# Attention probabilities split into halves in SBUF and transposed by DMA, in a cross-attention and two-expert network kernel

## The reference

```python
x = x + _L0_xattn_ref(_layernorm(x, axis=-1), ctx_1024, mask_Bx1xSxS2_ik0, mask_Bx1xS2_bk0, Wq, Wk, Wv, Wo, bo)
x = x + _L0_ffn_ref(_layernorm(x, axis=-1), gate_w, w1, b1, w2, b2, sw1, sb1, sw2, sb2)
# attention: sim = q k^T * SCALE, masked; attn = softmax(sim); out = attn v; out Wo^T + bo
# network: routing_output (relu network of the row's top-1 expert, plus the idle expert's bias path)
#          + shared (relu(xf @ sw1 + sb1) @ sw2 + sb2)
```

## Time and profile before

| | |
|---|---|
| median of 3 runs | 1881.85 us (1881.73 to 1882.95) |
| the profiled execution | 1883.23 us |
| its span | 1881.4 us |
| TensorE busy in the span | 1823.4 us, 97% |
| VectorE, ScalarE, GpSimd busy | 794.6, 821.2, 500.3 us |

### The profile page before, as it was taken

One profiled execution on the slowest core, in us unless ns is written; L12 is line 12 of the kernel. 1 busy time (PEld: TensorE's weight loads), 2 busy tenths in 40 slices (PEclk: granted clock), 3 DMA queues, 4 the chain that ended last, 5 costly groups with the idle time before them and its releaser, 6 DMA issues. The chain is left out here.

```text
span 1881.4 us, 33418 instructions
## 1 busy us (share of the span) xinstructions
PE 1823.4 (97%) x11516; PEld 1149.2 (61%) x11517; DVE 794.6 (42%) x1651; ACT 821.2 (44%) x1441; POOL 500.3 (27%) x475
## 2 busy tenths in 40 slices
PE   8989999999989999999999999999999999999997
PEld 6334444544656666666666666666666666666664
DVE  6977778777334343343433332222222222222222
ACT  3655555555333333335445544333333334333333
POOL 2047777776101111121100010222111121222111
PEclk9999999999989999999999999999999999999998
DMA  8235555555962333233345493812211112212100
GB/s 324 85 87 149 165 166 167 172 165 142 280 112 83 98 91 100 81 98 123 123 143 147 138 326 96 257 46 58 55 46 45 39 46 55 52 50 61 46 24 15
DMA packets 230151, 214.44 MB, mean 114 GB/s; under 512 B 130864, under 2 KB 172336, under 8 KB 229680
## 3 DMA queue, kind: packets, MB, share of 16 engines
q1 hardware_dynamic: 221120, 188.09, 34.9%
q0 software_dynamic: 8944, 25.19, 4.2%
HBM read 129.57 MB, written 59.02 MB: 100 GB/s over the span
## 5 line engine op out<-in xcount | busy, mean ns | idle before, releaser
L1058 PE MATMUL pS<-room_a,room_w 128*128 128x256 f16 (+1 forms) x6336 | 768.1, 272 | 8.4 <-issue 5.7
L1058 PEld LDWEIGHTS pS<-room_a,room_w 128*128 (+1 forms) x6336 | 612.9, 98 | 191.2 <-issue 18.0
L1089 DVE TENSOR_TENSOR room_a<-room_a 128x256 f16<-128x256 f32 (+1 forms) x528 | 235.2, 446 | 912.3 <-ACT room_a L1083 885.9
L1070 PE MATMUL pP<-room_w,room_a 128*128 (+1 forms) x1584 | 384.8, 380 | 9.2 <-DVE room_a L1089 9.2
L1081 ACT ACTIVATE room_a<-pS,room_b,sc 128x256 f32<-128x256 f32 (+1 forms) x272 | 151.7, 558 | 429.2 <-PE pS L1058 401.4
L1081 ACT ACTIVATE room_a<-pS,b1s,sc 128x256 f32<-128x256 f32 x256 | 144.2, 563 | 381.4 <-PE pS L1058 378.2
L1070 PEld LDWEIGHTS pP<-room_w,room_a 128*128 128x128 f16 x1584 | 155.0, 98 | 142.1 <-DVE room_a L1089 9.5
L1070 PE MATMUL pG<-room_w,room_a 128*128 128x512 f16 (+1 forms) x768 | 207.5, 379 | 0.4 <-DVE room_a L1089 0.4
L1070 PE MATMUL pO<-room_w,room_a 128*128 128x512 f16 (+1 forms) x768 | 207.6, 379 | 0.0
L1106 POOL TENSOR_TENSOR room_a<-room_a,room_b 128x512 f32<-128x512 f32 x32 | 42.7, 1354 | 535.8 <-DVE room_a L1097 535.8
L480 PE MATMUL pO<-room_w,room_b 128*128 (+1 forms) x768 | 172.7, 382 | 4.8 <-DVE room_b L692 4.7
(11 more groups left out here) (180 smaller groups left out, 1538.1 us busy)
## 6 DMA issues: line engine op xcount, KB each, us to landing
room_b<-in_w SPq DMA_DIRECT2D x64, 512.0 KB, 4.9
e_split<-room_b SPq DMA_DIRECT2D x64, 256.0 KB
room_w<-e_split SPq DMA_DIRECT2D x8, 2048.0 KB
rows_room<-in_x SPq DMA_DIRECT2D x32, 256.0 KB, 3.1
room_a<-in_sw SPq DMA_DIRECT2D x32, 256.0 KB, 4.3
room_b<-in_x SPq DMA_DIRECT2D x32, 256.0 KB, 4.1
s_split<-room_a SPq DMA_DIRECT2D x64, 128.0 KB, 3.8
x_scratch<-room_b SPq DMA_DIRECT2D x32, 256.0 KB, 4.2
```

The lines of the kernel that those rows point to most:

```text
L1058: mm = q.matmul(self.pH[j % 2][:, 0:rows], w[:, k, j * P:(j + 1) * P], zt[:, u, k, 0:rows], start=(n == 0), stop=(n == 3 * KC - 1))
L1070: mm = q.matmul(self.pY[u][r][:, :], h[:, j % self.HR, r * P:(r + 1) * P], w[:, j, :], start=(j == 0 and n == 0), stop=(j == HC - 1 and n ...
L1089: q.tensor_tensor(self.hl[:, j % self.HR, 0:rows], self.hf[:, j % self.HR, 0:rows], self.hh[:, j % self.HR, 0:rows], ALU.subtract).then_in ...
```

## The change

The transposes of the probabilities on TensorE and the identity go. `hi_p` and `lo_p` now read `s` in SBUF and write both halves side by side to `prs`; SyncE turns them with one DMA, `turn_p`, into `pT` (two buffers), and `attend` reads that. `hi_p` waits until the turn of the block before has been read out. On VectorE `lo_p` now stands ahead of `residual`; on SyncE `turn_p` stands first in a block's list, and `load_w1_w2(0)` moves behind the turn of the last block. For the first blocks, one `lo_x` and one `shifts` are placed earlier. The order list is blanked before the loop, from 33 rows of 128 zeros, and no longer from `inv`. Small buffers of the shared network change place, and VectorE waits for `lo_z` of block 30 (`z_done`) before it writes `rb1`.

```diff
+                prs = take([2, HEADS, KEYS], F16)
-                pTh = take([PAIRS, P], F16)
-                pTl = take([PAIRS, P], F16)
+                pT = take([2, 2 * PAIRS, P], F16)
...
+                    sp.wait_ge(S["zeros"], 1)
+                    sp.dma_start(order_d.rearrange("(s p) one -> s (p one)", p=P), zeros).then_inc(blank, 16)
...
+                    def turn_p(e, g, u):
+                        e.wait_ge(S["pl"], count(g, u))
+                        at_least(e, S["att"], count(g, u) - 2)
+                        e.dma_start(pT[:, u % 2, :, :], prs[:, :, :, :].rearrange("p l h k -> p (l h k)"), transpose=True).then_inc(S["pT_in", u % 2], 16)
...
                         for u in range(N):
+                            step(sp, g, u, 0, turn_p)
+                            if isinstance(g, int) and N * g + u == SUB - 1:
+                                sp.wait_ge(S["sim"], SUB)
+                                load_w1_w2(0)
                             step(sp, g, u, 3, turn_x)
...
                             snet.transpose(sp, t, z_d[t * TOK:(t + 1) * TOK, :])
-                        sp.wait_ge(S["sim"], SUB)
-                        load_w1_w2(0)
...
-                    def t_p(e, g, u):
-                        e.wait_ge(S["prob"], count(g, u))
-                        at_least(e, S["pTl"], count(g, u) - 1)
-                        for q in range(PAIRS):
-                            mm = e.transpose(pP[:, q * P:(q + 1) * P],
-                                             s[:, u % 2, 2 * q:2 * q + 2, :].rearrange("p h k -> p (h k)"), ident[:, :])
-                        mm.then_inc(S["pT"], 1)
-
                     def attend(e, g, u):
-                        e.wait_ge(S["pTl"], count(g, u))
+                        e.wait_ge(S["pT_in", u % 2], dma_count2(g, u))
...
-                            step(pe, g, u, 0, t_p)
                             step(pe, g, u, 2, sim)
                             step(pe, g, u, 0, attend)
...
                     def hi_p(e, g, u):
-                        e.wait_ge(S["pT"], count(g, u))
-                        at_least(e, S["att"], count(g, u) - 1)
-                        e.activation(pTh[:, :, :], pP[:, :].rearrange("p (k n) -> p k n", k=PAIRS), ACT.Copy, scale=P_SCALE).then_inc(S["pTh"], 1)
+                        e.wait_ge(S["prob"], count(g, u))
+                        if u > 0:
+                            e.wait_ge(S["pT_in", (u - 1) % 2], dma_count2(g, u - 1))
+                        elif not isinstance(g, int) or g > 0:
+                            e.wait_ge(S["pT_in", 1], 32 * g)
+                        e.activation(prs[:, 0, :, :], s[:, u % 2, :, :], ACT.Copy, scale=P_SCALE).then_inc(S["ph"], 1)
...
                     def body(g):
                         for u in range(N):
-                            if not early(g, u, 3):
+                            if not early(g, u, 3) and not first_tile(g, u, 1):
                                 step(pool, g, u, 3, lo_x)
...
+                            if first_tile(g, u, 2):
+                                step(pool, g, u, 4, lo_x)
...
                     def lo_p(e, g, u):
-                        e.wait_ge(S["pTh"], count(g, u))
-                        e.scalar_tensor_tensor(out=pTl[:, :, :], in0=pP[:, :].rearrange("p (k n) -> p k n", k=PAIRS), scalar=P_SCALE,
-                                               in1=pTh[:, :, :], op0=ALU.mult, op1=ALU.subtract).then_inc(S["pTl"], 1)
+                        e.wait_ge(S["ph"], count(g, u))
+                        e.scalar_tensor_tensor(out=prs[:, 1, :, :], in0=s[:, u % 2, :, :], scalar=P_SCALE,
+                                               in1=prs[:, 0, :, :], op0=ALU.mult, op1=ALU.subtract).then_inc(S["pl"], 1)
...
                         for u in range(N):
+                            step(dve, g, u, 0, lo_p)
                             step(dve, g, u, -1, residual)
-                            step(dve, g, u, 0, lo_p)
                             step(dve, g, u, 2, dropped)
...
                             if first_tile(g, u, 2):
                                 other_scales()
+                                step(dve, g, u, 4, shifts)
...
-        sp.wait_ge(S["inv0"], 1)
         slots_of = order_d.rearrange("(s p) one -> p (s one)", p=P)
-        with nc.allow_non_contiguous_dma("one slot per lane"):
-            sp.dma_start(slots_of, inv[:, :]).then_inc(S["blank"], 16)
...
+        dve.wait_ge(z_done, SUB - 1)
         dve.tensor_scalar(rb1[:, :], b1e[:, :], 0.0, None, ALU.max).then_inc(S["rb1"], 1)
```

More of the change, by code:

```diff
@@ L918, in body @@
                                 other_scales()
+                                step(dve, g, u, 4, shifts)
                             step(dve, g, u, 2, masked)
                             step(dve, g, u, -1, agg2_done)
-                            if not early(g, u, 4):
+                            if not early(g, u, 4) and not first_tile(g, u, 2):
                                 step(dve, g, u, 4, shifts)
@@ L933, in xattn_ffn @@
                 el = take([2, 2, DM], F16)
-                brow = take([DM])
-                take([DM])
-                cacc = take([2, DM])
+                small = room_b[:, 6240:6752]
+                brow, cacc = room_b[:, 7264:7776], room_b[:, 8288:9312].rearrange("p (e n) -> p e n", n=DM)
+                take = carve(small)
                 inv = take([SLOT_SUBS])
@@ L948, in xattn_ffn @@
                 snet.S["e_out"] = f.enter_context(nc.semaphore("s_e_out"))
-                room = (f, take, er, sc, wA, wB, room_w, cacc, order, inv, is1, is0, eh, el, iz, brow, w_in, snet, enet, stored, first_in)
+                room = (f, take, er, blank, sc, wA, wB, room_w, cacc, order, inv, is1, is0, eh, el, iz, brow, w_in, snet, enet, stored, first_in)
                 shared_sync, shared_tensor, shared_scalar, shared_gpsimd, shared_vector = shared_net(
@@ L992, with __init__ @@
     LAG = 2
-    def __init__(self, tag, count, sem, sc, ident, a1, a2, room, rows_room, banks, half=None):
-        self.tiles, self.ident, self.half = count, ident, half
+    def __init__(self, tag, count, sem, sc, a1, a2, room, rows_room, banks, half=None):
+        self.tiles, self.half = count, half
         self.a1, self.a2 = sc[:, a1:a1 + 1], sc[:, a2:a2 + 1]
@@ L1143, in shared_net @@
 def shared_net(nc, room, x1_d, z_d, res_d, order_d, split_s, split_e, units, w1, w2, sb2, net_scales, consts, cols):
-    f, take, er, sc, wA, wB, _, cacc, order, inv, is1, is0, eh, el, iz, brow, w_in, net, enet, stored, first_in = room
+    f, take, er, blank, sc, wA, wB, _, cacc, order, inv, is1, is0, eh, el, iz, brow, w_in, net, enet, stored, first_in = room
     ones, upper, lane, row_id, starts, b1e, b1e_s, b1s, expert1 = consts
@@ L1155, in sem @@
         S[n] = f.enter_context(nc.semaphore("s_" + n))
-    for n in ("brow_in", "e_am", "e_red", "e_step", "ranks", "sort", "inv0", "blank", "scattered", "inv_in", "ordered", "eh", "el", "cacc", "rb1", "seen"):
+    for n in ("brow_in", "e_am", "e_red", "e_step", "ranks", "sort", "scattered", "inv_in", "ordered", "eh", "el", "cacc", "rb1", "seen"):
         sem(n)
@@ L1485, in experts @@
 def experts(nc, room, room_b, z_d, res_d, out, split_e, b2, consts):
-    _, _, _, sc, wA, wB, room_w, cacc, order, inv, is1, is0, eh, el, iz, brow, w_in, snet, net, _, _ = room
+    _, _, _, _, sc, wA, wB, room_w, cacc, order, inv, is1, is0, eh, el, iz, brow, w_in, snet, net, _, _ = room
     ones, b1e_s = consts
```

35 lines of the change are left out of this document (15 added, 20 removed).

## The result

The changed kernel takes 1914.39 us, median of 4 runs (1910.81 to 1915.33), against 1882.22 (1881.73 to 1882.95) for the kernel before: ratio 1.0167, interval 1.015 to 1.0185, some 32 us slower. The forecast was 1906 in 1894 to 1926. The profiled execution after took 1913.93 us, with a span of 1912.2 against 1881.4: 30.8 more. These split at the first matmul of the shared network. It starts at 528.51 us, 43.9 later than before; what follows it takes 1383.7 us against 1396.8, 13.1 less. The prediction said +35.3 and -11.6. (Times in the profile, like these, are from the one profiled execution of a kernel.)

The account below looks back on a forecast made before the run. It took the ScalarE and VectorE circle to bind the changed loop, at 12.4 us a block. 1883.2 + 35.3 (later network start) - 11.6 (blanking) = 1906.9, as a median 1905.5, said as 1906; range 1894 to 1926.

Parts of the forecast that it names:

- (b): VectorE's low half moved ahead of the residual: the residual's and statistics' 1.40 us lengthen circle one, 10.82 to 12.22 us.
- circle one: Loop through VectorE and ScalarE: low half to last shift, normal2 and normal, hi_p, next low half; 10.82 us before.
- Rivals 4 and 5: Circle one does not bind, 1878 us, chance 0.07; or TensorE sets the pace, 1856 us, chance 0.09.
- (c): Both halves in SBUF: low half 0.08 us more, hi_p 0 to 0.14 more; period taken as 12.4 us.
- (d): Turn of p, one more DMA a block on SyncE: 2.5 us to issue, 4.4 to land, hidden.
- Rival 2: Turn of p lands late, in 7 us: TensorE's circle 13.0 us, 15 us more, 1921 us; chance 0.15.
- The serial reading: Turn of p moving sixteen tiles one after another: landing 21 us, block 20 us; not used in the sum.
- the stores' path: SyncE's queue: z stored 12.9 to 13.3 us after the low half, residual needs it at 13.6; hidden.
- (e): Loop start: low half of block 0 at 127.0, masked scores of block 3 at 143.4, low half of block 2 at 150.4.
- (f): Loop end: shared network starts 59.5 us after the low half of block 27, at 519.9 against 484.58, +35.3.
- (g): Order list blanked by one small DMA before the loop: expert-weight stall near the network's second tile goes, gain 11.6 us.

Follow-up runs that it names:

- b_lofirst: The kernel before with only VectorE's order changed, low half ahead of the residual, transposes still on TensorE: 1903.54 us, ratio 1.0128.
- a_psum: The changed kernel with the low half reading its first operand from cleared PSUM, its part left out of the result: 1899.79 us, ratio 1.0107.
- a_hiearly: The changed kernel with hi_p moved ahead of normal2 and normal on ScalarE, behind the weights' split: 1871.58 us, ratio 0.9955 against the kernel before.
- a_resfirst: The changed kernel with the residual back ahead of the low half on VectorE: 1963.85 us, ratio 1.0453 against the kernel before.
- a_swap: The changed kernel with the turn of p behind the turn of x on SyncE: 1935.15 us, ratio 1.0295 against the kernel before.
- b_blank: The kernel before with only the early blanking of the order list: 1869.8 us, ratio 0.9951; on another chip 1869.36 us, ratio 0.9937.
- a_oldblank: The changed kernel with the old blanking, one number at a time ahead of the second expert-weight load: 1925.5 us, ratio 1.0248 against the kernel before.

## Why the prediction was right, and where it was off

**(b), the low half ahead of the residual: right, and the largest part.** The forecast stood on circle one rising from 10.82 to 12.22. b_lofirst shows 12.06 from that edit alone, and a_psum 12.20 with the rest of the change beside it. The signs named came: low halves that wait for ScalarE about 3 us, TensorE idle before `attend`; only the low halves are 12.66 apart and not 12.3 to 12.5. That a_hiearly, which cuts this circle on ScalarE, takes the loop to 11.42 shows the same from the other side. Rivals 4 and 5 fell with it. What the prediction did not see is that the edit had a reason: with the turn of p on SyncE the old order costs 14.50 a block (a_resfirst).

**(c), both halves in SBUF: mis-sized.** I took 1.28 for the low half from the split of the expert weights, and 12.4 for the period. Busy time of the kernel before over that split, columns as in the earlier trace rows, shows GpSimd at 31.01 of 312 us, where in the loop it is at 170.81 of 240:

```profile
851.00:1163.00 312.00, 311.00 (x2147) 209.72 (x2145) 106.80 (x171) 153.75 (x270) 31.01 (x21) 1.00 0.51 160
```

And `lo_x` comes up at nearly the same moment as the low half. The low half took 1.71 on average over blocks 2 to 27, up to 2.25. Without that (a_psum) the period is 12.20, just under the 12.3 to 12.44 that I computed; with it 12.66. The row was right for the shape and the memories and wrong for the neighbour. Over 25 blocks the miss of 0.26 on the period is 6.5 us, most of the 8.6 by which the network started later than forecast.

**(d), the turn of p: right on landing, hidden as said.** 4.3 against 4.4, under the 5.8 from which it decides; the issue is 1.76 at the median, not 2.5. Rival 2 is out for this order; with the turn issued later (a_swap) something of its kind does reach the period. The serial reading weighed there, of the 1.309 us a tile that the Trainium skill gives in VectorE: DVE Perf Modes, The three transpose paths, did not hold: sixteen tiles in one DMA would take an estimated 21 us by it and landed in 4.3. The 0.3 to 0.7 to spare on the stores' path was enough: the residual waited once.

**(e), the start: 126.69 against 127.0, and block 2 at 152.01 against 150.4**, 1.6 late. `attend` of block 0, after 7.31 us without work, took 7.33 (row 132.53) where I had put 5.2, and `sim` of block 3 stands behind it: its masked scores came at 145.17, forecast 143.4. The granted clock is 0.50, the lower level, over 132.5 to 136 us, the first half of this `attend`, and 0.93 over the 4 us that follow. The term that failed is the duration after a long idle stretch, for which I had the 7.04 of the earlier trace rows and used it at the loop's end only.

**(f), the end: right in sum.** From the low half of 27 to the network it took 60.0 (forecast 59.5), and inside it the last turn went out at 47.9 (forecast 47) and `attend` of block 31 began at 52.5 (forecast 52.5), behind the z tiles as described. The prediction's words on its own sum, 28 or so for the period and 7 for the end, are off: by its terms it is 26.3 for the period (25 times 12.4 less 11.35), 10.4 for the end (59.5 less 49.1) and -1.4 for the start.

**(g), the blanking: right.** -13.1 behind the network's start, -11.6 said; b_blank gives 9.6 and 11.8, a_oldblank 11.1 from the other side (1925.5 less 1914.39; by the ratios 15).

**Sum.** +43.9 - 13.1 against +35.3 - 11.6: both terms too small in size, the larger by the stretched low half. The +43.9 are 0.2 at the start, 32.8 in the 25 periods and 10.9 at the end. The two misses have opposite signs, and 1.5 us of the 8.6 cancel; that much of the closeness is luck.

## What to carry to other kernels

An engine that is busy for over 99% of the loop hides the circles beside it: before taking work from it, add up, step by step, each loop that the in-order lists of the other engines close (here VectorE, ScalarE, VectorE at 10.82 against 11.23), and see which steps the edit puts in. A step moved to free one list can close another loop, and the remedy may be a third list: here one step moved on ScalarE took the change from 1.7% slower to 0.45% faster. The early blanking alone gives as much (0.5 to 0.6%), so the transposes by DMA, even with the circle opened, brought no gain of their own that the intervals show. And price an instruction from a row with the same neighbours: a VectorE instruction whose inputs both lie in SBUF was longer by up to 1 us when GpSimd worked beside it, and constant with one of them in PSUM.

## What the runs showed of the hardware

- The low half (two inputs of 128x1024, in SBUF) and `lo_x` on GpSimd (128x512): 1.21 to 1.23 and 1.16 us alone, and up to 2.25 and 2.15 for the one that starts second. With one input in PSUM, 1.22 and 1.16 in every block.
- One DMA with transpose of 128 x 2048 halves lands in 4.3 us, one of half the size in 3.1 to 3.6; with 1.76 and 1.78 us to issue at the median in the changed kernel. The smaller one takes 1.23 to issue where it is first in the list (before, and a_swap), and the larger one behind it then takes 2.05. Twice the tiles cost 0.7 to 1.2 us of landing.
- A DMA that writes 16.5 KB to DRAM in numbers of 4 bytes takes 19.3 us to land and the load behind it on the queue comes 13.56 us too late for VectorE; in rows of 512 bytes, ahead of the loop, nothing of it is seen.
- TensorE's granted clock is 0.96 over 200 to 440 us in the changed kernel, which idles before each `attend`, and 1.00 before, where it never does; at 1.00 it also is in a_psum, which idles as much (34.1 of 240 us, against 32.5). It set no time in the loop of the changed kernel, since TensorE is not in the circle that binds there.
- One `attend` takes 5.34 us at the upper clock level. It took 7.33 behind 7.31 us without work (block 0 of the changed kernel) and 8.31 behind 3.46 (a_swap), each with a granted clock of 0.50 in its first half.

The fastest complete kernel is b_blank, the one before with the blanking alone, at 1869.4 to 1869.8 us (ratios 0.9937 and 0.9951). a_hiearly, the changed kernel with one step moved, is at 0.9955, which the intervals can't tell from it.
